# Attention with a soft mixture of experts: turn groups merged, tile 4 cut in 320 and 320, the queries' slot read crosswise

## The reference, cut to what matters

```
x: (8, 1024, 128) f32; wq, wk, wv: (128, 8, 128); wo: (8, 128, 128)
q, k = rope(x @ wq), rope(x @ wk);  v = x @ wv                  # 8 batches, 8 heads
p = softmax(causal(q @ k.T / 128))
x = layernorm(x + sum over heads of (p @ v) @ wo)
x = layernorm(x + mixture_ffn(x))                               # slots, gelu, 8 x 64 experts' slots
```

## Time and profile before

| what | value |
|---|---|
| runs, us | 1763.75, 1767.71, 1769.49 |
| median, us | 1767.71 |
| the profiled execution, us | 1769.15 |
| its span in the trace, us | 1767.3 |
| TensorE (PE) busy | 1694.9 us, 96% |
| VectorE (DVE) busy | 1431.5 us, 81% |
| ScalarE (ACT) busy | 1237.6 us, 70% |
| GpSimd (POOL) busy | 1134.0 us, 64% |
| granted TensorE clock, mean | 0.99 |

### The profile page before, as it was taken

One profiled execution on the slowest core, in us unless ns is written; L12 is line 12 of the kernel. 1 busy time (PEld: TensorE's weight loads), 2 busy tenths in 40 slices (PEclk: granted clock), 3 DMA queues, 4 the chain that ended last, 5 costly groups with the idle time before them and its releaser, 6 DMA issues. The chain is left out here.

```text
span 1767.3 us, 33370 instructions
## 1 busy us (share of the span) xinstructions
PE 1694.9 (96%) x10524; PEld 1481.7 (84%) x10524; DVE 1431.5 (81%) x2945; ACT 1237.6 (70%) x2361; POOL 1134.0 (64%) x684
## 2 busy tenths in 40 slices
PE   5999999999999999999999999999999997999996
PEld 4788888888888888888888888888888886889886
DVE  4888988897889888977898889879889887677764
ACT  3777777776777777767777777777777763665663
POOL 4566666665666656666666666666666654677775
PEclk9999999999999999999999999999999999999999
DMA  4222232223222322232223222322232323123212
GB/s 143 65 61 77 73 101 61 76 73 86 66 74 73 100 67 73 73 97 73 73 73 96 73 73 73 96 73 72 72 85 72 85 73 93 46 62 94 60 31 54
DMA packets 76518, 134.23 MB, mean 76 GB/s; under 512 B 19264, under 2 KB 45888, under 8 KB 76352
## 3 DMA queue, kind: packets, MB, share of 16 engines
q1 hardware_dynamic: 74880, 130.10, 27.7%
q10 hardware_dynamic: 1472, 2.10, 0.4%
HBM read 56.36 MB, written 8.70 MB: 37 GB/s over the span
## 5 line engine op out<-in xcount | busy, mean ns | idle before, releaser
L493 ACT ACTIVATE probs<-ps_slot,neg_max 128x640 f32<-128x640 f32 (+7 forms) x512 | 378.7, 741 | 121.1 <-DVE neg_max L600 111.7
L600 DVE CUSTOM_DVE_ANT_0 ps_slot<-ps_slot,causal 128x640 f32<-128x640 f32 (+7 forms) x512 | 386.8, 756 | 58.1 <-PE ps_slot L57 57.3
L816 PE MATMUL ps_turn<-ident,probs 128*128 128x128 f32 x2304 | 338.8, 277 | 19.8 <-DVE x_t L657 6.3
L426 POOL TENSOR_TENSOR q<-rot_q,q 128x1024 fp32r<-128x1024 f32 x64 | 153.9, 2404 | 245.0 <-ACT q L510 245.0
L816 PEld LDWEIGHTS ps_turn<-ident,probs 128*128 128x128 f32 x2304 | 257.7, 141 | 51.6 <-DVE x_t L657 8.0
L55 PE MATMUL ps_slot<-k,q 128*128 128x512 f32 (+3 forms) x768 | 285.0, 371 | 2.7 <-DVE rot_q L616 1.5
L57 PE MATMUL ps_slot<-k,q 128*128 128x512 f32 (+3 forms) x768 | 267.8, 349 | 0.0
L56 PE MATMUL ps_slot<-k,q 128*128 128x512 f32 (+3 forms) x768 | 267.1, 348 | 0.0
L418 POOL TENSOR_TENSOR swapped_q<-swapped_q,rope 128x1024 f32<-128x1024 f32 x64 | 170.8, 2669 | 77.0 <-DMA swapped_q<-unrot_q 76.9
L426 POOL TENSOR_TENSOR k<-rot_k,k 128x1024 fp32r<-128x1024 f32 x64 | 153.1, 2392 | 82.3 <-ACT k L510 79.8
L527 ACT ACTIVATE pt_split<-ps_turn 128x512 fp32r<-128x512 f32 x256 | 145.2, 595 | 61.8 <-PE ps_turn L816 61.8
(11 more groups left out here) (168 smaller groups left out, 4348.6 us busy)
## 6 DMA issues: line engine op xcount, KB each, us to landing
swapped_k<-unrot_k SPq DMA_DIRECT2D x128, 256.0 KB, 3.6
swapped_q<-unrot_q SPq DMA_DIRECT2D x128, 256.0 KB, 3.7
inv_b<-inv_rows SPq DMA_DIRECT2D x64, 512.0 KB, 5.0
x_rows<-in_L_attn_x SPq DMA_DIRECT2D x8, 512.0 KB, 5.2
y_t<-y_sum SPq DMA_DIRECT2D x8, 512.0 KB, 5.2
x_rows<-y_t SPq DMA_DIRECT2D x8, 512.0 KB, 3.9
unrot_q<-in_L_attn_x SPq DMA_DIRECT2D x8, 512.0 KB, 5.4
row_b<-r_rows SPq DMA_DIRECT2D x16, 256.0 KB, 3.5
```

Of the source, the lines that this page charges most:

```text
L426: pool.tensor_tensor(out[:, 1, :], rot[which][:, :], f32(out[:, 0, :]), ALU.subtract)\
L493: act.activation(probs_tile(t), score_tile(name, head, i), ACT.Exp, scale=-1.0, bias=neg_max[:, head.par, t:t + 1], accum_out=sums[:, head ...
L600: dve.tensor_tensor_reduce(tile, tile, causal[:, T - WIDTH[t]:T], -1.0, UNSEEN, ALU.add, ALU.min, neg_max[:, head.par, t:t + 1]).then_inc( ...
L816: last = pe.transpose(bank[:, at:at + P], probs_tile(t)[:, j * P:(j + 1) * P], ident[:, :])
```

## The change

- `ps_turn`'s fills become ten: "10" of one head and "4b" of the next share one bank (`turn_shared`, with "4b" in the last 128 columns), one group of transpositions, one high-part and one low-part pass signal. With ten fills a fill always has the same bank.
- TensorE's order of transposition groups: "5a" directly behind "2", ahead of s4; "7b" behind s10, directly ahead of "6b". With "6a" and "5b", and "4a" and "7a", which were adjacent already, a head has five groups: (2, 5a), (3, 10, 4b), (7b, 6b), (6a, 5b), (4a, 7a).
- ScalarE: the first exponential of s32 goes behind the copies "4a" and "7a"; the keys' high part ahead of "7b"; tile 5's exponentials ahead of the copy "6b". VectorE: the low part of "2" ahead of the row maximum of tile 4, the values' low part ahead of the first row maximum of s32.
- The queries' slot is projected in halves, columns 512 to 1023 first. VectorE multiplies the second half first, while ScalarE copies the first one, then they change places. The semaphores `filled["q"]`, `raw_made[0]` and `cos_made[0]` count two per head.
- Tile 4's scores start at column 192 of the slot, so that the bank's border cuts them in 320 and 320 columns instead of 512 and 128.

```diff
               "s6": (6, 0), "s5": (7, 0), "s10": (8, 0)}
+SLOT_OFFSET = {"s4": 192}
 SLOT_TILES = {"s7": (7,), "s6": (6,), "s5": (5,), "s4": (4,), "s32": (3, 2), "s10": (1, 0)}
 NB_SLOT = len(SLOT_FILLS)
 
 
 TURN_FILLS = {"5b": (0, 1, (5, 4, 6)), "4a": (1, 1, (4, 0, 4)), "7a": (2, 1, (7, 0, 4)), "2": (3, 1, (2, 0, 3)),
               "5a": (4, 1, (5, 0, 4)), "3": (5, 1, (3, 0, 4)), "10": (6, 1, (1, 0, 2), (0, 0, 1)),
-              "4b": (7, 0, (4, 4, 5)), "7b": (8, 0, (7, 4, 8)), "6b": (9, 0, (6, 4, 7)), "6a": (10, 0, (6, 0, 4))}
-NB_TURN = len(TURN_FILLS)
-TURNS_OF_NO_HEAD = 7
+              "4b": (6, 0, (4, 4, 5)), "7b": (7, 0, (7, 4, 8)), "6b": (8, 0, (6, 4, 7)), "6a": (9, 0, (6, 0, 4))}
+NB_TURN = 10
+TURNS_OF_NO_HEAD = 6
+
+TURN_AT = {"4b": 3 * P}
...
-            return slot(name, head)[:, i * BANK:i * BANK + WIDTH[t]]
+            at = i * BANK + SLOT_OFFSET.get(name, 0)
+            return slot(name, head)[:, at:at + WIDTH[t]]
 
         def probs_tile(t):
             return probs[:, PROBS_AT[t]:PROBS_AT[t] + WIDTH[t]]
 
         def turn_bank(name, head):
-            return ps_turn[:, (head.at + TURN_FILLS[name][1] + TURN_FILLS[name][0]) % 2, :]
+            return ps_turn[:, TURN_FILLS[name][0] % 2, :]
 
         def turn_views(name, head, part):
 
-            at = 0
+            at = TURN_AT.get(name, 0)
...
 
-            def raw(which, head):
-                if not head.live():
-                    return
-                name = "qk"[which]
-                act.wait_ge(filled[name], head.made())
+            def raw_k(head):
+                if not head.live():
+                    return
+                act.wait_ge(filled["k"], head.made())
                 if head.step(-1).live():
-                    act.wait_ge(sin_made[which], head.step(-1).made())
-                act.activation(unrot[which][:, :], slot(name, head), ACT.Copy).then_inc(raw_made[which], 1)
+                    act.wait_ge(sin_made[1], head.step(-1).made())
+                act.activation(unrot[1][:, :], slot("k", head), ACT.Copy).then_inc(raw_made[1], 1)
+
+            def raw_q(head):
+                if not head.live():
+                    return
+                if head.step(-1).live():
+                    act.wait_ge(sin_made[0], head.step(-1).made())
+                act.wait_ge(filled["q"], head.made() * 2)
+                for place, half in enumerate((0, 1)):
+                    if place == 1:
+                        act.wait_ge(cos_made[0], head.made() * 2 - 1)
+                    act.activation(unrot[0][:, half_cols(half)], slot("q", head)[:, half_cols(half)],
+                                   ACT.Copy).then_inc(raw_made[0], 1)
...
+                last.then_inc(turn_hi, 1)
+
+            def turn_shared(before, head):
+                act.wait_ge(turned, head.turns("4b"))
+                if before.live():
+                    act.wait_ge(high_done, before.made())
+                    for hi, src in turn_views("10", before, 0):
+                        last = act.activation(hi, src, ACT.Copy)
+                if head.live():
+                    for hi, src in turn_views("4b", head, 0):
+                        last = act.activation(hi, src, ACT.Copy)
...
                 turn("4a", before)
                 turn("7a", before)
+                exp("s32", before, 1)
                 exp("s32", before, 0)
-                raw(1, after)
-                raw(0, after)
+                raw_k(after)
+                raw_q(after)
                 turn("2", before, low_done)
                 turn("5a", before)
...
+                turn_shared(before, head)
                 if is_step(head, heads):
                     act.wait_ge(z_turned, 1)
                     act.activation(kept.z_t[:, 0, :], z_slot, ACT.Copy).then_inc(z_hi, 1)
                 exp("s7", head)
                 exp("s6", head)
-                turn("4b", head, high_done)
+                split_hi(1, after)
                 turn("7b", head)
-                split_hi(1, after)
+                exp("s5", head)
                 turn("6b", head)
-                exp("s5", head)
                 exp("s10", head, 1)
                 exp("s10", head, 0)
...
             def mul_cos_q(head):
                 if not head.live():
                     return
-                dve.wait_ge(raw_made[0], head.made())
                 if head.step(-1).live():
                     dve.wait_ge(lo_made[0], head.step(-1).made())
-                dve.tensor_tensor(rot[0][:, :], slot("q", head), kept.rope[:, 0, :], ALU.mult).then_inc(cos_made[0], 1)
+                dve.wait_ge(filled["q"], head.made() * 2 - 1)
+                for place, half in enumerate((1, 0)):
+                    if place == 1:
+                        dve.wait_ge(raw_made[0], head.made() * 2 - 1)
+                    dve.tensor_tensor(rot[0][:, half_cols(half)], slot("q", head)[:, half_cols(half)],
+                                      kept.rope[:, 0, half_cols(half)], ALU.mult).then_inc(cos_made[0], 1)
 
             def rotate_add(which, head):
                 if not head.live():
...
                                       ALU.add).then_inc(tokens_added, 1)
+                turn("2", before)
                 rowmax("s4", head)
-                turn("2", before)
                 turn("5a", before)
...
                 else:
+                    split_v_lo(head)
                     rowmax("s32", head, 1)
-                    split_v_lo(head)
                 rowmax("s32", head, 0)
...
-            def project(which, head):
-                if not head.live():
-                    return
+            def project_half(which, head, half):
                 w = kept.w[:, head.no, :, :]
                 hi, lo = ((WQ_HI, WQ_LO), (WK_HI, WK_LO))[which]
                 xt = kept.x_t[head.at // 8 % 2]
-                name = "qk"[which]
-                for c in range(2):
-                    cols = slice(c * BANK, (c + 1) * BANK)
-                    last = matmul_split(pe, slot(name, head)[:, cols], w[:, hi, :], w[:, lo, :],
-                                        xt[:, 0, cols], xt[:, 1, cols], True, True)
-                last.then_inc(filled[name], 1)
+                cols = half_cols(half)
+                return matmul_split(pe, slot("qk"[which], head)[:, cols], w[:, hi, :], w[:, lo, :],
+                                    xt[:, 0, cols], xt[:, 1, cols], True, True)
+
+            def project_k(head):
+                if not head.live():
+                    return
+                project_half(1, head, 0)
+                project_half(1, head, 1).then_inc(filled["k"], 1)
+
+            def project_q(head, half):
+                if not head.live():
+                    return
+                project_half(0, head, half).then_inc(filled["q"], 1)
...
-                    for c0 in range(0, WIDTH[t], BANK):
-                        cols = slice(c0, min(c0 + BANK, WIDTH[t]))
+                    room = BANK - SLOT_OFFSET.get(name, 0)
+                    for cols in (slice(0, min(room, WIDTH[t])), slice(room, WIDTH[t])):
+                        if cols.start >= cols.stop:
+                            continue
                         last = matmul_split(pe, score_tile(name, head, i)[:, cols], q[:, 0, rows], q[:, 1, rows],
                                             k[:, 0, cols], k[:, 1, cols], True, True)
                 last.then_inc(filled[name], 1)
...
+            def turn_shared(before, head):
+                if before.live():
+                    for t, j0, j1 in TURN_FILLS["10"][2:]:
+                        pe.wait_ge(exped[t], before.made())
+                    pe.wait_ge(turn_lo, before.turns("5a"))
+                    at = 0
+                    for t, j0, j1 in TURN_FILLS["10"][2:]:
+                        for j in range(j0, j1):
+                            last = pe.transpose(turn_bank("10", before)[:, at:at + P],
+                                                probs_tile(t)[:, j * P:(j + 1) * P], ident[:, :])
+                            at += P
+                if head.live():
+                    pe.wait_ge(exped[4], head.made())
+                    last = pe.transpose(turn_bank("4b", head)[:, 3 * P:4 * P], probs_tile(4)[:, 4 * P:5 * P], ident[:, :])
+                last.then_inc(turned, 1)
+
             def turn_x(head, half):
...
-                project(1, after)
+                project_k(after)
+                free_slot(exped[2], before)
+                project_q(after, 1)
                 free_slot(exped[3], before)
-                project(0, after)
...
                 if head.live():
                     pe.wait_ge(lo_made[1], head.made())
...
-                turn("5a", before, ("7a", before))
-                free_slot(cos_made[0], after)
+                if after.live():
+                    pe.wait_ge(raw_made[0], after.made() * 2)
+                    pe.wait_ge(cos_made[0], after.made() * 2)
                 scores("s7", head)
```

(3 more changed lines are left out.)

39 lines of the change are left out of this document (24 added, 15 removed).

## The result

The changed kernel took 1763.95 us (median of 22 runs, 1760.12 to 1767.71), the kernel before in the same comparison 1767.8 (22 runs, 1763.58 to 1769.72). The ratio is 0.9983, with an interval of 0.9976 to 0.9990: some 3 us, or 0.17%, faster. That is within the 0.3% named above as no change; the forecast was 17 us faster. 1763.95 lies inside the stated range, near its slow end.

What follows compares the result with a forecast made beforehand. TensorE's issue plus short holds was taken to bound the attention stretch; heads falling from 21.84 to 21.58 save 0.26 us, over 64 heads 16.6 us, giving 1751 us, range 1737 to 1766.

Steps and rivals of the forecast that it cites:

- TensorE's holds and pieces: TensorE alone per head: holds of 0.10, 0.09, 0.19 go, tile 4 saves 0.09, groups 0.06; 21.72 becomes 21.19 us.
- the crosswise reading: Queries projected, copied and multiplied in halves: holds of 0.09 ahead of their product and 0.19 ahead of tile 7 go.
- the rival in which tile 4's pieces cost 0.23 each: Each 320-column product takes 0.23: 0.41 more, 0.15 over the hold that covers it, time 1760; chance 0.03.
- The collision and the chain behind it: Every keys' sum collides with GpSimd's queries product, ends at 17.84; ScalarE's queue then delays "5b", next projection at 21.54.
- I add 0.04 in the mean: Allowance for the queries' swap letting GpSimd begin later than 14.35 in some heads: head 21.54 becomes 21.58 us.
- the gain is used up from a start of 14.6 on: In the slower rival, GpSimd's queries product starting from 14.6 us into a head leaves no gain; beyond 15.2 nothing is lost.
- the slower rival: Swap lands just ahead of the keys' sum, GpSimd from 15.1: heads 22.3 us, 29 slower, time 1796; chance 0.09.
- The rival of no change: Tile 4's row maximum comes 0.35 us late and holds "4b" and all behind: heads 21.85, time 1768; chance 0.10.
- The mean ordinary head is ... 21.84 us: Kernel before: 0.51 of heads at 21.72 and 0.49 collided at 21.97 us, the base of the gain.
- The eight that also load the next batch counted alike: Heads that also load rows gain the same 0.26 us, so all 64 heads together gain 16.6 us.
- A group costs about 0.03. Two fewer give 0.06: TensorE's transposition groups: five groups instead of the former ones save 0.06 us per head; fewer signals and waits count nothing.
- I take 0.08: New wait of TensorE at "4b" for tile 4's exponentials, only just ready: priced 0 to 0.2, taken as 0.08 us.

Runs made afterwards that it cites:

- the third experiment: Changed kernel with ScalarE's old order at one place (7b copy, keys' high part, 6b copy, tile 5's exponentials): 1779.6 us, ratio 1.0055.

## Why the prediction was wrong

- **TensorE's holds and pieces: right.** Nothing waits ahead of the keys', the queries' product and tile 7, tile 4 costs 0.11 less, and each part, undone alone, costs about what its line in the sum said; for the crosswise reading that is partly luck (above). One slip of the working had no effect: the rival in which tile 4's pieces cost 0.23 each counts its 0.41 from the 1.06 of before, though 21.27 already has 0.09 less. Counted from there it is 0.50, or 0.23 over the hold, and the rival's time some 1766 instead of 1760.
- **The collision and the chain behind it: right.** All but two of the 49 ordinary heads collide, the mean sum over all 64 heads is 2.70 us, and the chain was walked to some hundredths in the heads with GpSimd from 14.36. The Trainium skill, SBUF — State Buffer, section "SBUF: two separate sides", has GpSimd and a VectorE instruction with two SBUF inputs exclude each other for a whole instruction, first come first served. The pairs of rows here agree: 2.74 and 3.35 behind GpSimd, 1.22 ahead of it, and so does the other pair (2.14 in the kernel before and 2.55 in the third experiment, behind GpSimd's low part of the keys). In all 53 collided heads of the changed kernel's 62 the sum ends 1.07 to 1.09 us after GpSimd.
- **"I add 0.04 in the mean": the step that failed.** It is the term for the swap's landing. The mean start is 14.68, 0.33 over 14.35, not 0.04 over it. By the line above that is 21.85 instead of 21.58, and 0.27 x 49 = 13 us. The prediction had the slope ("each tenth later lengthens the head by a tenth") and the edge ("the gain is used up from a start of 14.6 on"), and two landings 0.2 apart in its rows. It took 14.35 from one head. It gave the slower rival 0.09, with the words that every landing of before came within 0.2 of the edge; that reading was wrong, for in the trace of before GpSimd begins 15.35 to 17.21 us into the ordinary heads. That rival came true in part: 12 of the 49 heads collide with a start of 14.9 to 15.4 and take 22.1 to 22.5, where it said 22.3. The rival of no change had its condition met as well, in nine heads: the row maximum of tile 4 came 0.35 us late, though not for the reason given (last section), and TensorE waited 0.35 for it, at "10".
- **"The mean ordinary head is ... 21.84 us": 0.07 too low.** It is 21.91 in the trace of before. The changed kernel's heads are 0.24 over the forecast 21.58, so by this second error the gain per head is 0.09 and not 0.02.
- **"The eight that also load the next batch counted alike": wrong too.** These and the heads at the loop's turn got 3.6 us slower, where 2.8 were to be gained. The trace shows a part of it: two of the heads that load have a collided sum (18.08, 3.15 long) and take 24.91, three with the sum first take 23.93. Without the groups the eleven take 259.0, so it is again the groups that make them long in this kernel. But the groups alone, added to the kernel before, cost them only 0.9 us (265.3 against 264.4, each from a single profile): it takes the groups together with the other parts. What does so at each of these heads was not separated.
- **"A group costs about 0.03. Two fewer give 0.06": near in the restarts (0.04), wrong as a sum.** With no sum of the keys colliding, the groups cost 0.14 per head, in the waits that their order brings.
- **"I take 0.08" at "4b": not there.** The transposition "4b" starts 0.11 behind its neighbour, the usual pace, in all 49 heads. The wait is one step ahead, at "10": 0.03 us in most heads, 0.12 in the last eleven, 0.38 in the nine at places 5, 7 and 9.

The sum with measured terms: -4.2 (49 heads), +3.6 (11 heads), and the first two heads -2.6, together -3.2; but the first two differ by up to 5 us between the profiles here (44.0 to 48.9). The medians say -3.9, the ratio -3.0.

## What to carry to other kernels

When a step moves an operation next to one that excludes it, its start must be known as a distribution over all repeats, not from one: the cost is a cliff (here from 0.9 us when GpSimd starts just ahead of VectorE to nothing when it starts just behind), and a mean correction hides it. When a collision is in the trace, first try to make the less urgent engine wait for the urgent one: this single wait gave 9.5 us on the old kernel and 24 on the new one, though only about 4 where the room behind the collision was left (without the groups). And time the parts of a composite change apart; one of four took back 85% of what the others brought to an ordinary head.

## What the runs showed of the hardware that was not expected

The landing of the same swap, issued at the same 9.89 us of a head, varies by 1 us from head to head (14.2 to 15.2 in the changed kernel, and 15.6 in one head), and mostly in the same way at the same place of the loop of 16 (at places 5 and 7 GpSimd begins at 15.0 to 15.1 in all three turns, at place 6 at 14.35 to 14.37). The trace has something that goes with it: in these six heads, and in one at place 9 that landed at 15.19, a packet of 8 KB of the instruction queue q14 starts at 12.43 to 12.48, while the swap is on its way, and in no other ordinary head does one start then. No run moved that packet, one head landed late without one, and other instruction packets went by without a late landing, so this is an association and not a cause.

And at places 5, 7 and 9, in the changed kernel and in three of its variants (keys' sum first, ScalarE's old order, swap issued first), VectorE begins the row maximum of tile 4 about 0.35 us late. The changed kernel with keys' sum first, heads that began at 468.46 and 489.77: TensorE's last product of tile 4, and VectorE's row maximum behind it.

```profile
478.20 0.31 PE L57 MATMUL ps_slot<-k,q 128*128 128x320 f32 x1
...
499.51 0.31 PE L57 MATMUL ps_slot<-k,q 128*128 128x320 f32 x1
```

```profile
478.71 0.83 DVE L630 CUSTOM_DVE_ANT_0 ps_slot<-ps_slot,causal 128x640 f32<-128x640 f32 x1 [0.38 <-PE ps_slot L57]
...
500.36 0.83 DVE L630 CUSTOM_DVE_ANT_0 ps_slot<-ps_slot,causal 128x640 f32<-128x640 f32 x1 [0.73 <-PE ps_slot L57]
```

The last product starts at 9.74 in both heads, the row maximum at 10.25 and at 10.59; "10" then waits for it, and such heads take 21.66 instead of 21.31. In the changed kernel without the groups it begins at 9.81 or 9.82 in every ordinary head, and in the kernel with the groups alone no head is late either. The three turns repeat it, and TensorE's last product starts at the same time, so something that depends on the place in the code is likely, but no run took it away, and the cause of both stays open.
